# Second attention's scores stored pixel by pixel instead of neighbour by neighbour

## The chip, the cores and the metric

One core of a Trainium2 chip runs the kernel as one program. The metric is the device time of one execution in microseconds (us). A core has five engines that run side by side and meet at semaphores: TensorE (PE, matrix products; its weight loads are listed as PEld), VectorE (DVE), ScalarE (ACT), GpSimd (POOL) and SyncE (SP, which here only issues transfers).

## The reference

The input is x, 8 images of 16 x 16 pixels with 192 channels. Four blocks follow each other, each added to its own input:

1. a windowed attention (windows of 14 x 14, 12 heads of 16 channels);
2. a mixture of 8 experts over all 2048 tokens, two experts for each token;
3. the second attention, in which each pixel attends to nine neighbours;
4. a second mixture of experts.

The change touches the third. In the words of the reference, cut short:

```python
for g in range(4):                      # groups of 48 channels
    qkv = einsum('oi,bihw->bohw', qkv_w, xg[g])
    for i, dil in enumerate((1, 2, 3)): # heads of 16 channels
        kp, vp = unfold(k, 3, dil), unfold(v, 3, dil)   # nine shifted copies, zero beyond the edge
        attn = softmax(einsum('bncl,bnckl->bnlk', q, kp) * 16 ** -0.5, axis=-1)   # over the nine neighbours
        out  = einsum('bnlk,bnckl->bnlc', attn, vp)
y = stack(outs).reshape(B, H, W, C) @ proj_w.T + proj_b
```

For each pixel there are nine scores, each a dot product over 16 channels; softmax over the nine; and nine value vectors weighted by them.

## The kernel before, in words

**Layout of the second attention.** A partition holds one quarter of one image (4 rows of 16 pixels, QPIX = 64) of one group, 128 partitions in all, so one pass covers everything of one dilation. The three dilations are done in the order 3, 2, 1 (indices i = 2, 1, 0; "position" 0, 1, 2). Queries, keys and values lie as 16 channels by pixels, keys and values with a halo of rows above and below. The nine neighbours are in NEIGH, three of them (the three row offsets) to a column offset of 0, -1 and +1; for a column offset only those columns are computed that lie inside the image, so that an operation has 1024 elements for offset 0, and 960, 896 or 832 for the others at dilation 1, 2 or 3.

**Steps of one dilation**, and their engines:

- products (L1679, VectorE): query times shifted key, nine tensors of 16 channels x 64 pixels, one for each neighbour;
- channel_sums (L1795, TensorE): the 16 channels are added by 16 products with the identity matrix, into PSUM, 3 x 64 scores for each column offset;
- copy_scores (L1870, ScalarE): two copies, of 6 x 64 and 3 x 64 scores, from PSUM into the tile sc[i] of 576 numbers;
- scores (L1688 and L1690, VectorE): maximum over the nine, subtracted;
- exponentials (L1875, ScalarE): in place;
- weights (L1696, L1698, L1700, VectorE): sum over the nine, reciprocal, product;
- values (L1707, VectorE): for each neighbour, the shifted value window times its weights, repeated over the 16 channels. For dilation 3 nine such terms go straight to TensorE; for the other two, two of three terms of a column are first added on VectorE (L1737), so six go to TensorE. The terms have six buffers; a seventh waits for an older one's sum;
- neighbour_sums (L1813, TensorE): adds the terms into PSUM with the identity matrix;
- value_sums (L1881, ScalarE): copies the result into acc[i] with a pixel's 16 channels side by side, that is, writing with a step of 16 words.

**The order of the work** is written out by hand, one program for each engine, and an engine takes its instructions strictly in that order:

- VectorE: products of dilations 3 and 2, scores(2), the first column of products of dilation 1, weights(2), values(2), the other two columns of products, scores(1), weights(1), values(1), scores(0), weights(0), values(0);
- TensorE: channel_sums(2), channel_sums(1), neighbour_sums(2), channel_sums(0), neighbour_sums(1), neighbour_sums(0), then 24 filler products whose result nobody reads (L1848), then transposes (L1829) and the projection (L1842);
- ScalarE: copy_scores(2), exponentials(2), copy_scores(1), value_sums(2), exponentials(1), copy_scores(0), exponentials(0), value_sums(1), value_sums(0).

The SP queue stores acc[i] to DRAM after each value_sums, reads it all back in another order for the projection, and after that issues the loads of the second mixture's expert weights. Here position(i) = 2 - i.

Of the kernel before, what the change touches and what calls it, by code (L numbers as in the profile page):

```python
# [26 lines left out]
ALU = mybir.AluOpType  # L27
ACT = mybir.ActivationFunctionType
AX = mybir.AxisListType


P = 128
IMGS, SIDE, C = 8, 16, 192
# [50 lines left out]
def build(nc, a, out):  # L84

    ctx = ExitStack()
    with ctx:
# [3 lines left out]
        def sem(name):  # L91
            return ctx.enter_context(nc.semaphore(name))
# [51 lines left out]
        ps = ctx.enter_context(nc.psum_tensor("ps", [P, 8, 512], F32))  # L144
# [82 lines left out]
        def s_(name):  # L227
            if name not in S:
                S[name] = sem(name)
            return S[name]  # L230
# [69 lines left out]
        def block_scales(v, n, b):  # L300

            ln_refine(v, n, range(b, b + 1))
            nc.vector.scalar_tensor_tensor(offset[:, b], mv[:, b, :, 0], -1.0, rstd[:, b], ALU.mult, ALU.mult)\
                .then_inc(s_("ln_offset"), 1)
# [141 lines left out]
        for kind, b, start, end in sorted(misc_uses(), key=lambda use: use[2]):  # L446
            if start < len(FRONT):
                bank = start % 8
            else:
                bank = min((MISC, MISC + 1), key=lambda k: busy[k][0])  # L450
# [1083 lines left out]
        QPIX = QR * SIDE  # L1534
        QKV_UNITS = 12
        NEIGH = [(dy, dx) for dx in (0, -1, 1) for dy in (-1, 0, 1)]
        NN = len(NEIGH)
# [3 lines left out]
        def position(i):  # L1541

            return len(DIL) - 1 - i

        def halo(d):
            return QR + 2 * d

        def columns(d, dx):

            return max(0, -dx * d), SIDE - d * abs(dx)  # L1550
# [3 lines left out]
        for d in DIL:  # L1554
            n = HD * halo(d) * SIDE
# [15 lines left out]
        sc = [rt[:, i * NN * QPIX:(i + 1) * NN * QPIX] for i in range(3)]  # L1571
        mx1 = rt[:, 3 * NN * QPIX:3 * NN * QPIX + QPIX]
        sm1 = [rt[:, 3 * NN * QPIX + (1 + i) * QPIX:3 * NN * QPIX + (2 + i) * QPIX] for i in range(3)]
# [82 lines left out]
        def attn1_vector(v):  # L1656
            vec = nc.vector

            def shifted(t, i, n):

                d, (dy, dx) = DIL[i], NEIGH[n]
                x0, w = columns(d, dx)
                return t[i][:, :, d + dy * d:d + dy * d + QR, x0 + dx * d:x0 + dx * d + w]

            def in_columns(t, i, n):

                x0, w = columns(DIL[i], NEIGH[n][1])
                return t.rearrange("p c (y x) -> p c y x", x=SIDE)[:, :, :, x0:x0 + w]

            def products(i, col):  # L1670
                pos = position(i)
                if col == 0:
                    v.wait_ge(s_(f"q_in{i}"), 4 * 16)
                    v.wait_ge(s_(f"k_in{i}"), 4 * 16)
                if pos:
                    v.wait_ge(s_("qk_sum"), 3 * (pos - 1) + col + 1)
                x0, w = columns(DIL[i], NEIGH[3 * col][1])
                for n in range(3 * col, 3 * col + 3):
                    last = vec.tensor_tensor(in_columns(prod[:, n], i, n), q1[i][:, :, :, x0:x0 + w], shifted(k1, i, n), ALU.mult)  # L1679
                last.then_inc(s_("qk_prod"), 1)  # L1680

            def by_neighbour(s):
                return s.rearrange("p (n x) -> p n x", n=NN)

            def scores(i):
                pos = position(i)
                v.wait_ge(s_("sc_copied"), pos + 1)
                vec.tensor_reduce(mx1, sc[i].rearrange("p (n x) -> p x n", n=NN), AX.X, ALU.max).then_inc(s_("soft"), 1)  # L1688
                v.wait_ge(s_("soft"), pos + 1)
                vec.tensor_tensor(by_neighbour(sc[i]), by_neighbour(sc[i]), mx1.unsqueeze(1).broadcast_to([P, NN, QPIX]),  # L1690
                                  ALU.subtract).then_inc(s_("sc_ready"), 1)

            def weights(i):
                pos = position(i)
                v.wait_ge(s_("ex_ready"), pos + 1)
                vec.tensor_reduce(sm1[i], sc[i].rearrange("p (n x) -> p x n", n=NN), AX.X, ALU.add).then_inc(s_("norm"), 1)  # L1696
                v.wait_ge(s_("norm"), 3 * pos + 1)
                vec.reciprocal(sm1[i], sm1[i]).then_inc(s_("norm"), 1)  # L1698
                v.wait_ge(s_("norm"), 3 * pos + 2)
                vec.tensor_tensor(by_neighbour(sc[i]), by_neighbour(sc[i]), sm1[i].unsqueeze(1).broadcast_to([P, NN, QPIX]),  # L1700
                                  ALU.mult).then_inc(s_("norm"), 1)
                v.wait_ge(s_("norm"), 3 * pos + 3)

            def value_product(i, n, to):
                x0, w = columns(DIL[i], NEIGH[n][1])
                weight = sc[i][:, n * QPIX:(n + 1) * QPIX].rearrange("p (y x) -> p y x", x=SIDE)[:, :, x0:x0 + w]
                return vec.tensor_tensor(in_columns(to, i, n), shifted(v1, i, n),  # L1707
                                         weight.unsqueeze(1).broadcast_to([P, HD, QR, w]), ALU.mult)

            made, pairs = [0], [0]  # L1710

            def next_term():

                m = made[0]
                made[0] += 1
                if m >= TERMS:
                    v.wait_ge(s_("pv_sum"), m - TERMS + 1)
                return term[m % TERMS]

            def values(i):  # L1720
                v.wait_ge(s_(f"v_in{i}"), 4 * 16)
                if position(i) == 0:
                    for phase in range(3):
                        v.wait_ge(s_(f"qkv_out{phase}"), 16 * STORES)
                    for n in range(NN):
                        value_product(i, n, next_term()).then_inc(s_("pv_term"), 1)
                    return
                for col in range(3):
                    value_product(i, 3 * col + 2, next_term()).then_inc(s_("pv_term"), 1)
                    a_ = next_term()  # L1730
                    if pairs[0]:
                        v.wait_ge(s_("pv_term"), made[0] - 2)
                    value_product(i, 3 * col, a_)
                    value_product(i, 3 * col + 1, second_term).then_inc(s_("pair"), 1)
                    pairs[0] += 1
                    v.wait_ge(s_("pair"), pairs[0])
                    vec.tensor_tensor(in_columns(a_, i, 3 * col), in_columns(a_, i, 3 * col), in_columns(second_term, i, 3 * col),  # L1737
                                      ALU.add).then_inc(s_("pv_term"), 1)

            for i in (2, 1):  # L1740
                for col in range(3):
                    products(i, col)
            scores(2)
            products(0, 0)
            weights(2)
            values(2)
            products(0, 1)
            products(0, 2)
            scores(1)
            weights(1)  # L1750
            values(1)
            scores(0)
            weights(0)
            values(0)
            for u in range(2):
                vec.memset(rt[KC:KC + 1, u * 2 * BT:u * 2 * BT + BT], 1.0).then_inc(s_("y_ones"), 1)

            for b in range(BLKS):
                v.wait_ge(s_("proj1_mm"), b + 1)
                xs = x_sb[:, b * TPB:(b + 1) * TPB, :].rearrange("p (h t) c -> p h t c", h=2)  # L1760
                u = b % 2 * 2
                nc.vector.tensor_tensor(xs, xs, ps[:, u:u + 2, 0:2 * C].rearrange("p h (t c) -> p h t c", t=2), ALU.add)\
                    .then_inc(s_("proj1_out"), 1)
                v.wait_ge(s_("proj1_out"), b + 1)
                ln_moments(v, 3, range(b, b + 1))
                if b:
                    block_scales(v, 3, b - 1)
            block_scales(v, 3, BLKS - 1)
# [86 lines left out]
        def attn1_scalar(act):  # L1855
# [10 lines left out]
            def copy_scores(i):  # L1866
                pos = position(i)
                for bank, cols, count in ((SCORES[pos][0], slice(0, 6 * QPIX), 2), (SCORES[pos][1], slice(6 * QPIX, NN * QPIX), 3)):
                    act.wait_ge(s_("qk_sum"), 3 * pos + count)
                    last = nc.scalar.activation(sc[i][:, cols], ps[:, bank, 0:cols.stop - cols.start], ACT.Copy)  # L1870
                last.then_inc(s_("sc_copied"), 1)

            def exponentials(i):
# [3 lines left out]
            def value_sums(i):  # L1877
# [5 lines left out]
                    .then_inc(s_("acc_ready"), 1)  # L1883

            copy_scores(2)
            exponentials(2)
            copy_scores(1)
            value_sums(2)
            exponentials(1)
# [249 lines left out]
```

## Time and profile before

| | us |
|---|---|
| median of 3 runs (880.88 to 885.36) | 883.62 |
| the profiled execution, whole | 876.38 |
| its span | 874.6 |
| TensorE busy | 775.4 (89%) |
| VectorE busy | 419.6 (48%) |
| ScalarE busy | 308.2 (35%) |
| GpSimd busy | 363.2 (42%) |

The shares are averages over the whole program. The second attention's part from the first products of queries and keys to the last sum of values lies between 520 and 609 us of the span, and the rows are read from there. A line number (L1707) is that of the kernel; a mean is in ns, a start in us from the span's start. A busy matmul is not a TensorE at its peak, since matmuls are pipelined.

### The profile page before, as it was taken

The numbers are of one execution on the slowest core, as the hardware profiler recorded it, in microseconds if no ns is written. First come the engines' busy times: TensorE is split into PE (matmuls) and PEld (weight loads), VectorE is DVE, ScalarE is ACT, GpSimd is POOL, SyncE is SP. The second block draws the span as 40 slices with busy tenths as digits, with TensorE's granted clock in tenths as the row PEclk, the third lists the DMA queues.
The fourth block names the chain that finished last, engine by engine and source line by source line (L and its number), as shares of the span: only waits on it lengthen the run. The fifth ranks groups of instructions, "written<-read, shape, count | busy, mean of one in ns | idle before, by whom it ended". The sixth has DMA issues, their size and how long they took to land.

```text
span 874.6 us, 19316 instructions
## 1 busy us (share of the span) xinstructions
PE 775.4 (89%) x6126; PEld 660.1 (75%) x6127; DVE 419.6 (48%) x998; ACT 308.2 (35%) x858; POOL 363.2 (42%) x789
## 2 busy tenths in 40 slices
PE   8799999999987999999991589998967999999990
PEld 4577887888773999999990459783753999999980
DVE  5344455466648333333325427997347333333325
ACT  3403545555523333333340650011350333333330
POOL 8724343430132566666642030000033566666640
PEclk9855999999987999999996599999988999999995
DMA  7672565564482111111114089400980111111116
GB/s 235 189 170 79 116 171 133 138 148 89 160 334 86 46 48 49 42 51 52 47 35 145 7 252 216 68 25 28 322 336 25 43 51 46 49 48 47 49 24 216
DMA packets 60794, 96.50 MB, mean 110 GB/s; under 512 B 25679, under 2 KB 43812, under 8 KB 60744
## 3 DMA queue, kind: packets, MB, share of 16 engines
q1 hardware_dynamic: 43272, 61.56, 25.8%
q0 software_dynamic: 17472, 34.27, 13.2%
q8 instruction: 31, 0.51, 0.3%
q14 instruction: 19, 0.16, 0.1%
HBM read 65.51 MB, written 31.52 MB: 111 GB/s over the span
## 4 chain that ended last, share of the span: by engine, by line
PE 65%; DVE 15%; DMA 6%; issue 6%; POOL 4%; ACT 2%; SPq 1%; DVEq 0%; POOLq 0%
PE ps L1419 15%; PE ps L1427 11%; PE ps L1431 7%; PE ps L1795 4%; PE ps L754 3%; PE ps L779 3%; DVE x_sb L1359 2%; PE ps L730 2%; PE ps L1410 2%; PE ps L799 2%; PE ps L1813 2%; DVE arena L1707 2%; DMA kk<-kd 2%; PE ps L375 2%; PE ps L823 2%
## 5 line engine op out<-in xcount | busy, mean ns | idle before, releaser
L1461 ACT ACTIVATE arena<-ps,b1s 128x128 f32<-128x128 f32 x468 | 129.6, 375 | 254.1 <-PE ps L1431 170.2
L1419 PE MATMUL ps<-arena 128*128 x936 | 165.4, 327 | 1.5 <-DVE rt L1324 1.5
L1419 PEld LDWEIGHTS ps<-arena 128*128 128x128 f32 x936 | 150.3, 190 | 2.4 <-issue 2.1
L1427 PE MATMUL ps<-xnT 128*128 128x128 f32 x936 | 117.5, 275 | 3.8 <-DVE xnT L1317 3.8
L1427 PEld LDWEIGHTS ps<-xnT 128*128 128x128 f32 x936 | 114.4, 192 | 4.8 <-DVE xnT L1317 4.8
L272 POOL TENSOR_TENSOR rstd<-veps,cst 128x4 f32<-128x4 f32 (+1 forms) x12 | 14.9, 1239 | 189.7 <-DVE veps L266 189.6
L609 DVE TENSOR_REDUCE rt<-ps 98x2 f32<-98x392 f32 x96 | 53.2, 562 | 78.0 <-PE ps L779 78.0
L1475 POOL TENSOR_TENSOR credit<-credit 1x1 f32<-1x1 f32 x306 | 57.4, 187 | 77.0 <-DVE rt L1324 34.6
L1483 POOL DMA_INDIRECT xnT<-xnd,gcur x78 | 78.3, 1004 | 16.2 <-issue 15.2
L1026 ACT ACTIVATE arena<-ps 98x392 f32<-98x392 f32 x96 | 47.0, 499 | 76.6 <-PE ps L799 76.0
L1431 PE MATMUL ps<-xnT,rt 64*128 64x128 f32 x936 | 73.2, 289 | 0.0
L1493 POOL DMA_INDIRECT yd<-rt,scur x52 | 54.3, 1044 | 30.3 <-issue 30.3
L1331 DVE COPY xnT<-arena 128x768 f32 x78 | 44.5, 571 | 46.4 <-issue 45.6
L1431 PEld LDWEIGHTS ps<-xnT,rt 64*128 64x128 f32 x936 | 58.3, 187 | 9.4
L1317 DVE COPY xnT<-ps 128x256 f32<-128x256 f32 x78 | 33.1, 424 | 64.7 <-PE ps L1411 63.4
L1324 DVE TENSOR_TENSOR rt<-ps,xn 128x192 f32<-128x192 f32 x52 | 18.6, 358 | 82.2 <-issue 43.3
L779 PE MATMUL ps<-kk,qq 114*98 114x196 f32 x192 | 46.1, 328 | 6.4 <-DMA kk<-kd 6.2
L1795 PE MATMUL ps<-arena,cst 128*128 128x192 f32 x288 | 48.8, 333 | 3.1 <-DVE arena L1679 3.1
L1795 PEld LDWEIGHTS ps<-arena,cst 128*128 128x128 f32 x288 | 48.4, 195 | 3.9 <-DVE arena L1679 3.6
L754 PEld LDWEIGHTS ps<-xnT,arena 128*112 128x112 f32 (+2 forms) x448 | 40.0, 183 | 7.4 <-POOL xnT L554 4.1
L754 PE MATMUL ps<-xnT,arena 128*112 128x32 f32 (+4 forms) x448 | 42.2, 269 | 3.2 <-POOL xnT L554 3.2
L779 PEld LDWEIGHTS ps<-kk,qq 114*98 114x98 f32 x192 | 29.1, 189 | 16.5 <-issue 14.4
(211 smaller groups left out, 1278.6 us busy)
## 6 DMA issues: line engine op xcount, KB each, us to landing
arena<-in_w SPq DMA_DIRECT2D x16, 576.0 KB, 11.2
arena<-in_w1a SPq DMA_DIRECT2D x16, 384.0 KB, 6.0
arena<-yd SPq DMA_DIRECT2D x8, 768.0 KB, 7.1
kk<-kd SPq DMA_DIRECT2D x48, 96.0 KB
qq<-qd SPq DMA_DIRECT2D x16, 264.0 KB
qq<-qd SPq DMA_DIRECT2D x16, 192.0 KB
arena<-in_w1b SPq DMA_DIRECT2D x16, 192.0 KB, 6.3
qkvd<-arena POOLq DMA_DIRECT2D x8, 384.0 KB, 8.0
```

The lines of the kernel that those rows point to most:

```text
L609: m = nc.vector.tensor_reduce(mxa[0:WAH, cc, 2 * u:2 * u + 2, j], ps[0:WAH, SM + u, 0:2 * WA].rearrange("p (q n) -> p q n", q=2), AX.X, AL ...
L754: last = mm(o, relt[w][0:rows, at, 0:cols], q, start=True, stop=True)
L779: last = mm(ps[0:WAH, SM + u, c * WA:(c + 1) * WA], q[:, at:at + WAH], k[:, u * WA:(u + 1) * WA], start=True, stop=True)
L1026: e = nc.scalar.activation(pa[H % EXPS][0:WAH, u], ps[0:WAH, ST + n % 2, 0:2 * WA], ACT.Exp)
L1419: last = mm(ps[:, DOWN, 0:C], hidT[r][:, f, :], w2s[:, e, f, :], start=f == 0, stop=f == FT - 1)
L1427: mm(hidden(r, f), wcura[r][:, f * P:(f + 1) * P], xgT[:, 0, :], start=f < 2, stop=False, skip_group_check=True)
L1431: last = mm(hidden(r, f), wcurb[r][rows, f // 2 * P:(f // 2 + 1) * P], xgT[rows, 1, :], start=False, stop=f >= FT - 2, skip_group_check=True)
L1461: last = nc.scalar.activation(hidT[r][:, f, :], hidden(r, f), ACT.Gelu, bias=b1s[l][:, bass.ds(e * FT + f, 1)])
L1475: nc.gpsimd.tensor_tensor(credit[0:1, 12 + kind:13 + kind], credit[0:1, 0:1], credit[0:1, 0:1], ALU.add)\
L1483: nc.gpsimd.indirect_dma_start(out=xg[r], out_offset=None, in_=xnd[l], in_offset=bass.IndirectOffsetOnAxis(ap=gcur[:, r:r + 1], axis=0))\
L1493: nc.gpsimd.indirect_dma_start(out=yd[l], out_offset=bass.IndirectOffsetOnAxis(ap=scur[:, r:r + 1], axis=0), in_=ys[r], in_offset=None, bo ...
L1795: last = mm(to.rearrange("p (n x) -> p n x", n=3), ident, prod[:, 3 * col:3 * col + 3, c, :], start=c == 0, stop=c == HD - 1)
```

## The change

The tile sc[i] of 576 numbers keeps its size and place. Before, the number of neighbour n and pixel x is at n * 64 + x; after, at x * 9 + n. All that read or write it follow: ScalarE's two copies write it through a view that steps by nine words; the two reductions read nine adjacent words for each pixel; subtraction and normalisation repeat the pixel's maximum or factor nine times innermost instead of the whole row of 64 nine times; the value products read the weights of one neighbour nine words apart. The exponential runs over the whole tile as before. No instruction is added, removed or moved, and no wait is changed.

```diff
-            def by_neighbour(s):
-                return s.rearrange("p (n x) -> p n x", n=NN)
+            def by_pixel(s):
+                return s.rearrange("p (x n) -> p x n", n=NN)
...
-                vec.tensor_reduce(mx1, sc[i].rearrange("p (n x) -> p x n", n=NN), AX.X, ALU.max).then_inc(s_("soft"), 1)
+                vec.tensor_reduce(mx1, by_pixel(sc[i]), AX.X, ALU.max).then_inc(s_("soft"), 1)
                 v.wait_ge(s_("soft"), pos + 1)
-                vec.tensor_tensor(by_neighbour(sc[i]), by_neighbour(sc[i]), mx1.unsqueeze(1).broadcast_to([P, NN, QPIX]),
+                vec.tensor_tensor(by_pixel(sc[i]), by_pixel(sc[i]), mx1.unsqueeze(2).broadcast_to([P, QPIX, NN]),
                                   ALU.subtract).then_inc(s_("sc_ready"), 1)
...
-                vec.tensor_reduce(sm1[i], sc[i].rearrange("p (n x) -> p x n", n=NN), AX.X, ALU.add).then_inc(s_("norm"), 1)
+                vec.tensor_reduce(sm1[i], by_pixel(sc[i]), AX.X, ALU.add).then_inc(s_("norm"), 1)
...
-                vec.tensor_tensor(by_neighbour(sc[i]), by_neighbour(sc[i]), sm1[i].unsqueeze(1).broadcast_to([P, NN, QPIX]),
+                vec.tensor_tensor(by_pixel(sc[i]), by_pixel(sc[i]), sm1[i].unsqueeze(2).broadcast_to([P, QPIX, NN]),
                                   ALU.mult).then_inc(s_("norm"), 1)
...
-                weight = sc[i][:, n * QPIX:(n + 1) * QPIX].rearrange("p (y x) -> p y x", x=SIDE)[:, :, x0:x0 + w]
+                weight = sc[i].rearrange("p (y x n) -> p n y x", n=NN, x=SIDE)[:, n, :, x0:x0 + w]
...
-                    last = nc.scalar.activation(sc[i][:, cols], ps[:, bank, 0:cols.stop - cols.start], ACT.Copy)
+                    n0, n1 = cols.start // QPIX, cols.stop // QPIX
+                    last = nc.scalar.activation(sc[i].rearrange("p (x n) -> p n x", n=NN)[:, n0:n1],
+                                                ps[:, bank, 0:cols.stop - cols.start].rearrange("p (n x) -> p n x", n=n1 - n0),
+                                                ACT.Copy)
```

## Rows read from the trace of the kernel before

**Rows 1.** The page's chain that ended last: shares by engine, and by line.

```profile
PE 65%; DVE 15%; DMA 6%; issue 6%; POOL 4%; ACT 2%; SPq 1%; DVEq 0%; POOLq 0%
PE ps L1419 15%; PE ps L1427 11%; PE ps L1431 7%; PE ps L1795 4%; PE ps L754 3%; PE ps L779 3%; DVE x_sb L1359 2%; PE ps L730 2%; PE ps L1410 2%; PE ps L799 2%; PE ps L1813 2%; DVE arena L1707 2%; DMA kk<-kd 2%; PE ps L375 2%; PE ps L823 2%
```

**Rows 2.** That chain in order of time, 545 to 640: start, us, what.

```profile
556.32 13.65 PE ps L1813 x36
...
606.78 1.88 PE ps L1813 x4
608.66 10.30 PE ps L1848 x24
```

**Rows 3.** Stages: length, busy us (x) of PE, PEld, DVE, ACT, POOL, PEclk, DMA, GB/s.

```profile
556.00:570.00 14.00, 14.00 (x40) 7.15 (x40) 14.00 (x15) 0.35 (x2) 0.00 (x0) 1.00 0.00 0
570.00:585.00 15.00, 15.00 (x94) 15.00 (x93) 13.59 (x15) 2.90 (x3) 0.00 (x0) 1.00 0.09 36
...
598.00:608.00 10.00, 8.28 (x19) 3.53 (x20) 9.63 (x10) 0.00 (x0) 0.00 (x0) 1.00 0.13 53
```

**Rows 4.** VectorE's timeline, 540 to 610: start, us, operation, count, idle before.

```profile
547.91 3.50 DVE L1679 TENSOR_TENSOR arena<-pk,kk 128x1024 f32<-128x1024 f32 x3 [1.23 <-DMA kk<-qkvd]
551.32 1.14 DVE L1696 TENSOR_REDUCE rt<-rt 128x64 f32<-128x576 f32 x1
...
553.88 9.11 DVE L1707 TENSOR_TENSOR arena<-qq,rt 128x1024 f32<-128x1024 f32 x9
562.90 6.49 DVE L1679 TENSOR_TENSOR arena<-pk,kk 128x960 f32<-128x960 f32 x6
569.32 1.14 DVE L1688 TENSOR_REDUCE rt<-rt 128x64 f32<-128x576 f32 x1
...
575.01 3.50 DVE L1707 TENSOR_TENSOR arena<-qq,rt 128x1024 f32<-128x1024 f32 x3
...
587.94 1.14 DVE L1688 TENSOR_REDUCE rt<-rt 128x64 f32<-128x576 f32 x1
```

**Rows 5.** ScalarE's timeline, 530 to 625, columns as before.

```profile
569.99 1.95 ACT L1881 ACTIVATE arena<-ps 128x1024 f32<-128x1024 f32 x1 [13.30 <-PE ps L1813]
571.74 0.67 ACT L1875 ACTIVATE rt<-rt 128x576 f32<-128x576 f32 x1
...
585.59 0.33 ACT L1870 ACTIVATE rt<-ps 128x192 f32<-128x192 f32 x1 [4.71 <-PE ps L1795]
```

**Rows 6.** VectorE's groups by shape: busy us, mean ns, idle before and releaser.

```profile
L1707 DVE TENSOR_TENSOR arena<-qq,rt 128x1024 f32<-128x1024 f32 x9 | 10.5, 1220 | 0.1
...
L1707 DVE TENSOR_TENSOR arena<-qq,rt 128x832 f32<-128x832 f32 x6 | 5.7, 1019 | 0.0
...
L1696 DVE TENSOR_REDUCE rt<-rt 128x64 f32<-128x576 f32 x3 | 3.4, 1143 | 1.9 <-ACT rt L1875 1.9
L1688 DVE TENSOR_REDUCE rt<-rt 128x64 f32<-128x576 f32 x3 | 3.4, 1137 | 0.0
...
L1690 DVE TENSOR_TENSOR rt<-rt 128x576 f32<-128x576 f32 x3 | 2.3, 759 | 0.1
```

**Rows 7.** Groups by shape of nearby operations, VectorE's two, then ScalarE's two.

```profile
L609 DVE TENSOR_REDUCE rt<-ps 98x2 f32<-98x392 f32 x96 | 53.2, 562 | 78.0 <-PE ps L779 78.0
...
L1239 DVE TENSOR_TENSOR rt<-rt 128x128 f32<-128x128 f32 x4 | 1.2, 291 | 0.1
...
L1881 ACT ACTIVATE arena<-ps 128x1024 f32<-128x1024 f32 x3 | 5.8, 1930 | 29.5 <-PE ps L1813 29.5
...
L1870 ACT ACTIVATE rt<-ps 128x192 f32<-128x192 f32 x3 | 1.0, 332 | 14.1 <-PE ps L1795 14.1
```

**Rows 8.** Stages, for the granted clock (the number after POOL's), columns as Rows 3.

```profile
48.00:72.00 24.00, 23.61 (x106) 19.79 (x105) 8.91 (x17) 3.09 (x9) 7.74 (x10) 0.50 0.56 131
520.00:523.00 3.00, 0.17 (x1) 0.00 (x0) 3.00 (x3) 0.59 (x1) 0.52 (x1) 1.00 1.02 416
523.00:526.00 3.00, 2.69 (x8) 2.70 (x9) 3.00 (x5) 0.00 (x0) 0.00 (x0) 0.51 1.03 418
```

## The prediction

> **What bounds the kernel now.** I read four views in order: the chain of waits, the same chain in order of time around the second attention, a table of busy time by stage there, and VectorE's own timeline. The chain as a whole is a TensorE chain (65%), with VectorE at 15%, and the value products' line L1707 is only 2% of it [rows 1]. That share says little about this change: the time of one stage counts. In the stage the chain names TensorE until 569.97 us [rows 2] and then goes over mostly to VectorE, until the last TensorE sum at 606.78 us. The table shows why the chain's naming must be read with care: from 556 to 570 us both TensorE and VectorE are busy for 14.00 of 14.00 us [rows 3], so there are two chains side by side, and the one on VectorE is the one that goes on: its next instruction, L1688 at 569.32, follows its products without a gap [rows 4], and does not wait for the TensorE sums that end at 569.97. From 570 to 608 us VectorE is busy for 13.59 of 15 and 9.63 of the last 10 us [rows 3], and its only wait there for another engine is for ScalarE's exponential, 1.9 us in all [rows 6]. So VectorE, from L1696 at 551.32 to the last addition at about 606.75, is one string of work with almost no slack. What is added to it is added to the kernel.
>
> **What the change does to each operation.** The scores (576 numbers per partition: 9 neighbours by 64 pixels) are now stored pixel by pixel.
>
> *The two reductions.* Before, each reads a pixel's nine scores 64 words apart: 1.14 us for 576 elements [rows 6]. The nearest reduction in sequence, L609, takes 562 ns for 392 elements (out of PSUM, which is why I allow it 0.02 us either way) [rows 7], and the two shapes of L1707 give VectorE's rate: (1220 - 1019) / 192 = 1.047 ns an element [rows 6]. 576 in sequence: 562 + 184 x 1.047 = 755 ns. Each reduction loses 0.39 us, and the strided read is priced by the same rows: (1140 - 755) / 576 = 0.67 ns an element more.
>
> *Subtraction and normalisation.* The broadcast operand now has its repeat innermost. L1239 compares 128 elements with an operand repeated eight times innermost, in 291 ns; from L1690 (759 ns for 576) down at 1.047 ns an element, 128 elements would be 290 ns [rows 6, 7]. So no change: 0.76 us stays. Bounds: 0 both ways to within 0.01 us. The exponential runs over 576 adjacent numbers before and after: 0.
>
> *ScalarE's copies of the scores* now write with a step of nine words. The nearest row is L1881, which writes with a step of 16 words: 1930 ns for 1024, where its rate for adjacent writes, 332 ns for 192 and 0.83 ns each, gives about 1025; 0.88 ns an element more [rows 7]. The last copy of each attention (192 elements) grows by 0.17 us, the first by 0.34 us. All are covered: VectorE comes to the scores of dilation 1 at 587.94, and the copy ended at 585.92 [rows 4, 5]; the other two copies have more cover. These 2.0 us grow if VectorE gets later. Cost 0; without cover 0.17 us each.
>
> *The value products.* 27 of them, each a multiplication of a shifted value window by the weights of one neighbour, repeated over 16 channels: 9 of 1024 elements and 6 each of 832, 896 and 960. They run at 1.22 us for 1024 and 1.02 us for 832, 1.05 ns an element beyond the fixed part [rows 6], with odd and even window offsets alike. After the change the weights are nine words apart, every element a jump. No row of before has VectorE reading with such a step in one of two operands. Bounds: below, 0 (the second operand's port hides it, since its words are used again for each channel); above, the ScalarE row's 0.88, and since no row tells what a small step costs VectorE, I leave room up to twice the reduction's price, 1.34 ns an element. I take 0.67 ns, that of the reduction's row, because it is the only row of the same engine, reading, with jumps that leave no two adjacent words. The elements: dilation 3 comes first with 3 x 1024 + 6 x 832 = 8064, then dilation 2 with 8448, then dilation 1 with 8832; together 25,344. Extra: 5.4 + 5.7 + 5.9 = 17.0 us.
>
> The Trainium skill, page "Vector Engine (DVE) Microarchitecture Reference", section 5.2 (Measured stream behaviour on trn2), says the same of the mechanism: a port keeps its full rate only on runs of at least two adjacent words, and one source that jumps at every element makes it 1.73 ns instead of 1.054. It also says that small non-adjacent steps cost more than large ones, with 2.50 ns for steps of 24 words in both sources; no row here shows that for VectorE. By that figure, my estimate from the page would be an extra of 1.45 ns an element and 36.7 us instead of 17.0.
>
> **The sum along VectorE's string.** Scores of dilation 3: the reduction's gain is lost, because products(0, 0) behind it waits for a transfer until 547.91 anyway [rows 4]. Weights of dilation 3: -0.39; products +5.40, their end moves from 562.90 to 567.9. Here TensorE sums the terms at about 1.5 us each from 556.3 on and finishes at 569.97 [rows 2]; the last term now arrives at 567.9 and its sum takes 1.4 to 1.5 us, so TensorE still ends at about 570 and channel_sums(0) is not late. The six products behind, which the weights don't touch, shift by 5.0 us: the next scores start at 574.3 instead of 569.32. There -0.39 for each of two reductions, and ScalarE's exponential, which started at 571.74 right behind the value copy of 569.99 to 571.94 although its input was ready at 571.25 [rows 5], finds ScalarE free: -0.45. Products of dilation 2: +5.66. Scores and weights of dilation 1: -0.78. Products of dilation 1: +5.92. Total 16.98 - 5 x 0.39 - 0.45 = +14.6 us at the last addition. The wait for a free buffer of the six terms never bites: the sums it asks for are older than two terms.
>
> **What is late next: TensorE's clock.** The sums now wait for VectorE. Between the last term of dilation 2 (597.4) and the first of dilation 1 (603.7) TensorE has work for 1.9 us and then nothing for about 4. After 3.1 us of nothing, at 520.17 to 523.30, the granted clock went from 1.00 to 0.51 (from 2.4 to 1.2 GHz) [rows 8]. At 1.2 GHz the last sum (four matmuls, 1.88 us [rows 2]) would take some 1.6 us more, and the 24 filler matmuls behind it (10.30 us) up to 1.5 us more if the clock comes back as it did after 526; if it had come back before, nothing. I take 1.0 us between 0 and 3.1. From the last sum on, ScalarE's copy, the stores and reloads through DRAM, the projection and the whole second mixture of experts follow and shift without change; the SP queue that loads the expert weights stands behind the reload of the values, so no transfer starts early.
>
> Sum: +14.6 + 1.0 = +15.6 us. The profiled execution took 876.38 us (span 874.6 and 1.8 around it): 892.0. The median of the three runs is 883.62, 7.2 above the profiled one; I expect the same offset, so 883.62 + 15.6 = 899.2 us.
>
> **Rivals.**
>
> *The small step costs more than the large one (25%).* For it: in this trace ScalarE's step of 16 words costs 0.88 ns an element while VectorE's step of 64 costs 0.67, two engines, so the step itself is not separated; against: no VectorE row has it. With 0.88 the products cost 22.3 us and the kernel +20.9, 904.5; with twice the reduction's price, 34.0 us and +32.6, 916.2. Every other step of the sum stays. By the figure for steps of 24 words on the Trainium skill's page named above it would be +35.3, an estimate again.
>
> *The weight port hides the step, not slower than before (8%).* Place: L1707. The weights of a channel are the same 64 words 16 times over and only one of three streams jumps. If this costs nothing, what is left are the reductions, -0.39 three times: the gain on scores(1) is eaten by ScalarE's copy until 571.94 [rows 5], so -0.39 for the weights there and -0.78 for dilation 1. The last addition moves by -1.2, and the time is 882.4: not slower. The point from which it decides: with less than 0.05 to 0.09 ns an element (1.2 to 2.4 us over 25,344) there is no loss, and with less than about 0.25 ns none that a measurement can tell. Against it: the reduction has one stream that jumps too, and pays.
>
> *TensorE hides the first part (4%).* Reading the chain of waits literally, the products of dilation 3 are off it and their 5.0 us are free: +10.6, 894.2. Against: VectorE is 14.00 of 14.00 us busy there [rows 3].
>
> *TensorE's clock stays low through the sums and the fillers (8%).* From 48 to 72 us it was granted 0.50 although TensorE was busy for 23.61 of 24 us [rows 8], so it does not always come back at once. Then the last sum costs 1.6 and the fillers 10.3 more instead of 1.0: +26.5, 910.1.
>
> **How the numbers follow.** Forecast 55%, the four rivals as above. A change of under 0.5% (4.4 us) can't be told from none by a measurement of this kernel. Only the hidden port leads there, and part of an intermediate price: same 0.09. Nothing gives a gain of 4.4 us (all that the edit can save is 2.4 to 3): faster 0.01. Slower 0.90. The range begins at 890 (0.67 cut to a half, or a lower median) and ends at 919, so that it holds nearly all of the price up to twice the row.
>
> **What would show it.** L1707 rows of 1024 elements at about 1.91 us and of 832 at 1.58; L1688 and L1696 at 0.75; L1690 and L1700 unchanged; L1870 at 0.83 and 0.50; VectorE without a gap from 551 to about 621; L1848 starting near 623 instead of 608.66, and granted clock under 1.00 at some place between 600 and 610. Wrong if L1707 keeps 1.22 us (hidden port) or takes over 2.2 us (step price), or if the last sum moves by another amount than VectorE's own busy time grows by.

## The result

The changed kernel takes 898.14 us (median of 4 runs, 889.22 to 900.03), the one before 882.25 (875.02 to 885.36): ratio 1.0188, 95% interval 1.0136 to 1.0240. Timed again beside other runs of the kernel before it was 897.22 (6 runs), ratio 1.0201 (1.0154 to 1.0248). The ratios of 1.019 and 1.020 are some 17 us; forecast were +15.6 us and 899.2.

### The profile page after: what moved, and what is told of

It is laid out like the page before. It is cut to its first block, busy times and chain, and to the rows that moved or that the text cites. A ratio compares the mean times of both kernels' runs of the same rounds, so it can differ in the third digit from the quotient of the medians.

```text
span 896.7 us, 19316 instructions
## 1 busy us (share of the span) xinstructions
PE 789.8 (88%) x6126; PEld 667.0 (74%) x6127; DVE 435.9 (49%) x998; ACT 310.3 (35%) x858; POOL 364.3 (41%) x789
## 4 chain that ended last, share of the span: by engine, by line
PE 60%; DVE 17%; issue 6%; DMA 6%; POOL 5%; SPq 3%; ACT 2%; DVEq 0%; POOLq 0%
PE ps L1419 14%; PE ps L1427 10%; PE ps L1431 7%; DVE arena L1707 4%; PE ps L754 3%; DVE x_sb L1359 2%; PE ps L779 2%; PE ps L730 2%; PE ps L1410 2%; SPq L1606 2%; PE ps L375 2%; PE ps L799 2%; PE ps L823 2%; DMA qkvd<-arena 1%; PE ps L865 1%
## 5 line engine op out<-in xcount | busy, mean ns | idle before, releaser
L1813 PE MATMUL ps<-arena,cst 128*128 128x512 f32 (+3 forms) x84 | 38.9, 610 | 14.8 <-DVE arena L1737 11.7
L1707 DVE TENSOR_TENSOR arena<-qq,rt 128x1024 f32<-128x1024 f32 (+3 forms) x27 | 48.1, 1848 | 0.1
```

## The profile after

The profiled execution took 898.54 us, its span 896.7. First VectorE's groups by shape in the changed kernel, in the columns of [rows 6] and against them.

```profile
L1707 DVE TENSOR_TENSOR arena<-qq,rt 128x1024 f32<-128x1024 f32 x9 | 17.5, 2002 | 0.1
L1707 DVE TENSOR_TENSOR arena<-qq,rt 128x960 f32<-128x960 f32 x6 | 10.9, 1870 | 0.0
...
L1707 DVE TENSOR_TENSOR arena<-qq,rt 128x896 f32<-128x896 f32 x6 | 10.3, 1775 | 0.0
L1707 DVE TENSOR_TENSOR arena<-qq,rt 128x832 f32<-128x832 f32 x6 | 9.5, 1668 | 0.0
...
L1690 DVE TENSOR_TENSOR rt<-rt 128x576 f32<-128x576 f32 x3 | 2.3, 758 | 0.1
...
L1688 DVE TENSOR_REDUCE rt<-rt 128x64 f32<-128x576 f32 x3 | 2.3, 752 | 0.0
L1696 DVE TENSOR_REDUCE rt<-rt 128x64 f32<-128x576 f32 x3 | 2.3, 751 | 1.5 <-ACT rt L1878 1.5
```

The value products grew from 1220 to 2002 ns for 1024 elements and from 1019 to 1668 for 832. With 1151 and 1084 ns before for 960 and 896 elements the sum is 9 x 0.782 + 6 x (0.719 + 0.691 + 0.649) = 19.4 us over 25,344 elements: 0.765 ns an element. The reductions fell to 0.75 us, the elementwise operation kept 758 ns. ScalarE's copies of the scores, its two groups:

```profile
L1871 ACT ACTIVATE rt<-ps 128x384 f32<-128x384 f32 x3 | 2.6, 872 | 23.2 <-PE ps L1795 23.2
...
L1871 ACT ACTIVATE rt<-ps 128x192 f32<-128x192 f32 x3 | 1.6, 525 | 13.0 <-PE ps L1795 13.0
```

The groups of the kernel before that [rows 6] and [rows 7] leave out, for both comparisons:

```profile
L1707 DVE TENSOR_TENSOR arena<-qq,rt 128x960 f32<-128x960 f32 x6 | 6.6, 1151 | 0.0
L1707 DVE TENSOR_TENSOR arena<-qq,rt 128x896 f32<-128x896 f32 x6 | 6.2, 1084 | 0.0
...
L1870 ACT ACTIVATE rt<-ps 128x384 f32<-128x384 f32 x3 | 1.5, 492 | 26.5 <-PE ps L1795 26.5
```

The copies grew by 0.38 and 0.19 us, 1.0 ns an element. Now VectorE's timeline of the changed kernel, in the columns of [rows 4].

```profile
551.87 3.50 DVE L1679 TENSOR_TENSOR arena<-pk,kk 128x1024 f32<-128x1024 f32 x3 [1.74 <-DMA kk<-qkvd]
555.28 0.74 DVE L1696 TENSOR_REDUCE rt<-rt 128x64 f32<-128x576 f32 x1
...
557.44 15.26 DVE L1707 TENSOR_TENSOR arena<-qq,rt 128x1024 f32<-128x1024 f32 x9
572.60 6.51 DVE L1679 TENSOR_TENSOR arena<-pk,kk 128x960 f32<-128x960 f32 x6
579.01 0.76 DVE L1688 TENSOR_REDUCE rt<-rt 128x64 f32<-128x576 f32 x1
...
581.31 0.75 DVE L1696 TENSOR_REDUCE rt<-rt 128x64 f32<-128x576 f32 x1 [0.75 <-ACT rt L1878]
...
583.48 5.86 DVE L1707 TENSOR_TENSOR arena<-qq,rt 128x1024 f32<-128x1024 f32 x3
...
605.17 0.75 DVE L1696 TENSOR_REDUCE rt<-rt 128x64 f32<-128x576 f32 x1 [0.75 <-ACT rt L1878]
```

I measure the stage from the start of weights(2), L1696, to the start of the last sum of values. Before it ran from 551.32 [rows 4] to 606.78 [rows 2], 55.46 us. The chain in order of time of the changed kernel ends it at 627.55:

```profile
557.44 15.26 DVE arena L1707 x9
...
627.55 1.88 PE ps L1813 x4
629.43 10.30 PE ps L1848 x24
```

627.55 - 555.28 = 72.27 us, 16.8 more. The chain now goes through L1707 at 557.44 in one piece, where before it went through TensorE's sums: the string that was off the chain on the page has become the chain. The last sum (1.88 us) and the fillers (10.30 us) are as long as before [rows 2]. Within the stage VectorE waits for another engine only at ScalarE's exponentials of dilations 2 and 1, 0.75 us each (1.20 and 0.75 before), and never for TensorE.

The two profiled spans lie 22.1 us apart, more than the stage explains. Of the rest 4.0 us lie ahead of weights(2) (555.28 against 551.32), where nothing was changed, and 1.3 behind the last sum (269.2 against 267.8 us to the end). The second profile of the kernel before, below, has its weights(2) at 555.54, so the 4.0 us are spread between executions and not the change's. The 1.3 us are a spell of low TensorE clock that other kernels of this set have too, as told below.

## The experiments

All stages are as defined above. Timed ratios are against the kernel before on the same chip.

**Value products read adjacent words.** In the changed kernel:

```diff
-                weight = sc[i].rearrange("p (y x n) -> p n y x", n=NN, x=SIDE)[:, n, :, x0:x0 + w]
+                weight = sc[i][:, n * QPIX:(n + 1) * QPIX].rearrange("p (y x) -> p y x", x=SIDE)[:, :, x0:x0 + w]
```

> The changed kernel, but the value products read 64 adjacent words of the scores tile (so each neighbour gets the wrong weights; nothing else is left out). Stage from the start of weights(2), its reduction, to the start of the last sum: 55.46 us before, 72.27 after. Theory (all of the loss is VectorE's nine-word step in the value products): L1707 back at 1.22 us for 1024, stage 54.3 us (the reductions' gain, 0.39 three times), kernel 1 us under the one before, ratio 0.999. Rival (ScalarE's slower copies or a lower TensorE clock carry part of the loss): stage over 56 us and the kernel slower than before by 2 us or more.

VectorE's and then TensorE's timeline of this kernel give the ends of the stage:

```profile
547.92 0.74 DVE L1696 TENSOR_REDUCE rt<-rt 128x64 f32<-128x576 f32 x1
```

```profile
602.29 1.88 PE L1813 MATMUL ps<-arena,cst 128*128 128x480 f32 x4 [0.91 <-DVE arena L1737]
```

The products are back at 1221 ns for 1024 elements, and the stage is 602.29 - 547.92 = 54.37 us: the whole loss is gone, with ScalarE's slower copies still in place, so the copies carry no part of it. The five reductions inside the stage save 1.95 us; 0.84 of it goes to a longer wait for the exponential of dilation 2 (2.04 us instead of 1.20), and 1.1 is left. This run does not separate TensorE's clock, which did not fall inside its stage; that the clock carries no part of the stage follows from the changed kernel's timeline above, in which VectorE never waits for TensorE. The total did not follow: ratio 1.0070 (1.0038 to 1.0103) over 12 runs, which on its face is the rival's number. The excess does not lie in the stage: from the start of the last sum to the end it took 277.9 us instead of 267.8. The stages of this kernel behind the projection (granted clock is the number after POOL's):

```profile
630.00:632.00 2.00, 0.10 (x1) 0.00 (x0) 1.97 (x6) 1.89 (x5) 0.48 (x1) 1.00 1.03 413
...
634.00:652.00 18.00, 18.00 (x81) 17.23 (x79) 0.51 (x4) 6.18 (x13) 5.83 (x8) 0.50 0.81 301
```

After a pause of TensorE of 1.93 us (to 632.03) the clock fell to 0.50 (from 2.4 to 1.2 GHz) and stayed there for 18 us in which TensorE was busy for 18.00.

**The same kernel and the one before, profiled again.**

> The changed kernel with the value products reading adjacent words (wrong weights), once more: its stage was 54.4 us, 1.1 under the one before, yet 12 timed runs were 0.4 to 1.0% over it. In its profile TensorE's granted clock was 0.50 from 632 to 662 us although TensorE was busy all the time, and from the start of the last sum to the end it took 277.9 us instead of 267.8. Theory (whether that low clock falls there differs from execution to execution of one kernel): stage again 54.4, the rest again between 267 and 279, not necessarily 278. Rival (a fixed cost of this kernel): 277.9 within 0.5.

> The kernel before, profiled once more. Theory (the stage is fixed by VectorE's string, what lies ahead of it and behind it moves with the clock): stage 55.5 us within 0.7, start of weights(2) anywhere from 548 to 556 us, the rest from the last sum 267 to 278. Rival (the parts outside the stage are fixed for this kernel): 551.3 and 267.8 again.

The stages were 53.7 and 55.3 us, the rest 274.4 and 267.9, and weights(2) began at 547.32 and 555.54. The stage repeats; the first one is 0.7 us shorter than in this kernel's first profile because the wait for the exponential was 1.39 us and not 2.04. What lies ahead moves by 4 us, as expected. The rest of the first kernel, 274.4, lies in the range of the theory (267 to 279) and not at the rival's 277.9, with a granted clock of 0.50 once more from about 631.4 us, for some 13 us. For the kernel before, the rival's 267.8 came again and its 551.3 did not.

The spell belongs to no single kernel. From the end of the fillers to the end of the span it took 255.6 to 255.8 us in seven of the twelve profiles of this document. In the other five it took 257.0 (changed kernel, first profile), 258.7 (ScalarE turns the weights, below), 262.2 and 265.7 (this kernel), and 265.8 (the first run on steps, below). In these five the clock fell at the same pause of TensorE, 1.93 us long and some 30 us behind the start of the last sum; in the seven it stayed at 1.00 over that pause. Two falls in two profiles, worth 6.6 and 10.1 us, would account for a timed ratio of 1.007 with a shorter stage, but no timed run outside a profile shows its stages. What decides whether the clock falls there is open, and the timed ratio of this kernel says nothing about the stage.

**Only the value products read with the step.** In the kernel before, the same line the other way round:

```diff
-                weight = sc[i][:, n * QPIX:(n + 1) * QPIX].rearrange("p (y x) -> p y x", x=SIDE)[:, :, x0:x0 + w]
+                weight = sc[i].rearrange("p (y x n) -> p n y x", n=NN, x=SIDE)[:, n, :, x0:x0 + w]
```

> The kernel before, with only the value products reading with a step of nine (so the weights are permuted; nothing else is left out). Theory: L1707 at 2.00 us for 1024 and 1.67 for 832 as in the changed kernel, 19.4 us more of VectorE; stage 55.5 + 19.4 - 0.45 (ScalarE free for the exponential of dilation 2) = 74.4 us, ratio to before 1.021. If the price came from the whole new layout and not from this read alone, L1707 would be under 2 us and the stage under 72.

```profile
L1707 DVE TENSOR_TENSOR arena<-qq,rt 128x1024 f32<-128x1024 f32 x9 | 17.4, 1994 | 0.1
...
L1707 DVE TENSOR_TENSOR arena<-qq,rt 128x832 f32<-128x832 f32 x6 | 9.5, 1651 | 0.0
...
L1696 DVE TENSOR_REDUCE rt<-rt 128x64 f32<-128x576 f32 x3 | 3.4, 1138 | 1.5 <-ACT rt L1875 1.5
```

The groups by shape show the products as slow as in the changed kernel, with the reductions at their old 1.14 us. Stage 629.77 - 555.62 = 74.15 us, ratio 1.0264 (1.0219 to 1.0309). The read alone is the price; the layout's other edits only take 1.9 us off it. The ratio is higher than the 1.021 expected. Against the first profile of the kernel before, the span is 24.6 us longer: 4.3 us lie ahead of weights(2), 18.7 in the stage, and 1.7 in the last sum, at a clock of 0.50, and the fillers, which ended 13.87 us after its start instead of 12.18. How the timed runs divide is not known.

**Only ScalarE's copies write with the step.** In the kernel before, copy_scores of the changed one.

> The kernel before, with only ScalarE's two score copies writing with a step of nine (softmax then works on permuted scores; nothing else is left out). Theory: copies of 0.87 and 0.53 us instead of 0.49 and 0.33, all hidden: stage 55.5 us, ratio 1.000. Rival (they hold up the scores): stage 55.9 us or more.

Copies of 0.88 and 0.53 us, ratio 0.9977 (0.9931 to 1.0023), stage 56.1 us, which is the rival's side by my own bound. The trace puts the 0.6 us elsewhere: TensorE's sums of dilation 3 began 5.44 us after weights(2) here, 4.83 before and 4.65 in its second profile, all set by when the transfers of keys arrived. Where VectorE is quick, its exponential of dilation 2 waits for ScalarE, and ScalarE for those sums. The copies themselves ended 1.8 us or more before VectorE came for them. VectorE's wait for that exponential was 1.65 us (1.20 and 1.01 in the two profiles before) and the products of dilation 3 took 9.26 us instead of 9.11, which makes up the 0.6. So the bound was too tight, and no wait for the copies is seen.

**Only dilation 3 reads with the step.** In the changed kernel, behind the line of the weights:

```diff
+                if i < 2:
+                    weight = sc[i][:, n * QPIX:(n + 1) * QPIX].rearrange("p (y x) -> p y x", x=SIDE)[:, :, x0:x0 + w]
```

> The changed kernel with the step of nine in the value products of dilation 3 alone; dilations 2 and 1 read 64 adjacent words (wrong weights there). Theory (VectorE's string sets the end although TensorE is busy all the time): extra 3 x 0.78 + 6 x 0.65 = 6.2 us of products, less 5 x 0.39 and 0.45: stage 59.3 us, 3.8 over before, ratio 1.005. Rival (TensorE's sums of dilation 3 hide them, as the chain of waits has it): stage 54.3 us, ratio 0.999.

VectorE's timeline of it:

```profile
552.53 0.74 DVE L1696 TENSOR_REDUCE rt<-rt 128x64 f32<-128x576 f32 x1
...
569.85 6.48 DVE L1679 TENSOR_TENSOR arena<-pk,kk 128x960 f32<-128x960 f32 x6
576.26 0.73 DVE L1688 TENSOR_REDUCE rt<-rt 128x64 f32<-128x576 f32 x1
```

The products of dilation 3 take 15.2 us instead of 9.0 (553.88 to 562.90 in [rows 4]), and the next scores start 23.7 us after weights(2), before 18.0. TensorE was busy all that time, its sums of dilation 3 took 14.4 us instead of 13.65, and none of it hid VectorE's 5.7 us: stage 611.71 - 552.53 = 59.18 us, ratio 1.0036 (0.9996 to 1.0076). Both chains ran side by side, and the one off the printed chain was the one that counted.

**What a step costs.** In the kernel before, the 27 products read x instead, each with a step of its own:

```diff
+                def stepped(k):
+                    return flat[:, 0:QPIX * k].rearrange("p (y x k) -> p k y x", k=k, x=SIDE)[:, 0, :, x0:x0 + w]\
+                        .unsqueeze(1).broadcast_to([P, HD, QR, w])
...
+                if (i, n) == (1, 1):
+                    return vec.tensor_tensor(out_, in_, stepped(4), ALU.mult)
```

> The kernel before, with the 27 value products reading their weights from x instead of the scores, each with its own step: for 1024 elements steps of 1, 2, 3, 4, 8, 9, 16, 24 words and pairs of adjacent words 18 apart; for the narrower shapes 1, 2, 3, 4, 5, 6, 8, 9, 12, 16, 24, 32, 48. Theory A (any read that leaves no adjacent pair costs the same): all steps from 2 on cost 0.7 to 0.8 ns an element, pairs nothing. Theory B (the distance matters, small steps cost more, as the step of 64 words cost the reduction 0.67 and the step of nine 0.77): a slope or bumps over the steps, with 24 words at 1 ns or more. Theory C (what counts is whether two successive reads fall in one group of four words): steps of 2 free or half price, 3 in between, 4 and above full price.

Groups of 1024 elements, from the top with steps of 24, 4, 9, 16, 3 and 2 words:

```profile
L1759 DVE TENSOR_TENSOR arena<-qq,x_sb 128x1024 f32<-128x1024 f32 x1 | 2.7, 2711 | 0.0
...
L1739 DVE TENSOR_TENSOR arena<-qq,x_sb 128x1024 f32<-128x1024 f32 x1 | 2.0, 2029 | 0.0
...
L1755 DVE TENSOR_TENSOR arena<-qq,x_sb 128x1024 f32<-128x1024 f32 x1 | 2.0, 1981 | 0.0
...
L1757 DVE TENSOR_TENSOR arena<-qq,x_sb 128x1024 f32<-128x1024 f32 x1 | 1.9, 1873 | 0.0
...
L1737 DVE TENSOR_TENSOR arena<-qq,x_sb 128x1024 f32<-128x1024 f32 x1 | 1.6, 1579 | 0.0
...
L1716 DVE TENSOR_TENSOR arena<-qq,x_sb 128x1024 f32<-128x1024 f32 x1 | 1.2, 1218 | 0.0
```

A step of two words is free, three words cost 0.35 ns an element, four 0.79. That is theory C for the small steps; theory A falls with steps 2 and 3, and theory B has only the dear step of 24 for it. For both runs on steps there is one execution each, and the means are read, not the totals.

> The kernel before, with the value products reading their weights from x (so the values are wrong; nothing is left out): full-width products (1024 elements) in pairs of words, given as first word and distance inside the pair, pairs 16 words apart: (0,1), (3,1), (0,2), (0,3), (1,1), (2,2), and steps of 20, 28, 40; the narrower ones with steps 7 to 47. Theory (VectorE pays 0.6 to 0.8 ns an element unless two successive reads fall in one aligned group of four words): (0,1), (0,2), (0,3), (1,1) free at 1.22 us, (3,1) and (2,2) 1.9 us or more. Rival (adjacent pairs on an even word are what counts): (0,1) alone free, (0,2) and (0,3) at full price, (1,1) about 0.25 ns. For the steps: 24 is alone in being dear, or all of 20 to 28 are.

Here the pairs decided. A pair is written as first word and distance, so (3,1) reads words 3 and 4. Groups of 1024 elements, from the top: step 20; pairs (2,2), (3,1), (0,3), (1,1).

```profile
L1758 DVE TENSOR_TENSOR arena<-qq,x_sb 128x1024 f32<-128x1024 f32 x1 | 2.3, 2279 | 0.0
...
L1744 DVE TENSOR_TENSOR arena<-qq,x_sb 128x1024 f32<-128x1024 f32 x1 | 2.0, 1970 | 0.0
...
L1724 DVE TENSOR_TENSOR arena<-qq,x_sb 128x1024 f32<-128x1024 f32 x1 | 1.9, 1946 | 0.0
...
L1740 DVE TENSOR_TENSOR arena<-qq,x_sb 128x1024 f32<-128x1024 f32 x1 | 1.2, 1227 | 0.0
L1742 DVE TENSOR_TENSOR arena<-qq,x_sb 128x1024 f32<-128x1024 f32 x1 | 1.2, 1226 | 0.0
```

Words 0 and 3 of an aligned group of four, and words 1 and 2, cost nothing, as do (0,1) and (0,2) at 1224 and 1216 ns; words 3 and 4, adjacent but in two groups, cost 0.71 ns an element. So two successive reads in one aligned group of four words (16 bytes) run at full rate, adjacent or not, and reads that each open a new group pay. The step of three fits: of four successive reads three open a new group, halfway between the free pairs (two of four) and the full price (four of four), and it cost 0.30 to 0.35, about half of 0.71. How much depends on the distance, from both kernels and the shapes they have (ns an element over the adjacent read):

```
step in words   1, 2   3          4 to 12      14    16         18    20         21 to 23     24         25    26
extra ns        0.00   0.30-0.35  0.74-0.79    0.70  0.64-0.66  0.75  0.86-1.03  1.07-1.12    1.18-1.46  1.14  0.96
step in words   28         30    32    36    40         44    47, 48
extra ns        0.79-0.87  0.83  0.74  0.76  0.88-0.91  0.79  0.71
```

The Trainium skill bears on both: "SBUF — State Buffer" (section Specifications (TRN2), the row on cachelines) has lines of 16 bytes that want at least two hits, and the pairs agree; "Vector Engine (DVE) Microarchitecture Reference", section 5.2, has adjacent pairs on an even word as the condition, and the free pairs (0,3) and (1,1) contradict it. Its 2.50 ns for steps of 24 words in both sources is reached here with one stepped source at 1024 elements, 1.047 + 1.455 = 2.50; at 960 elements the same step gives 1.047 + 1.18 = 2.23.

**ScalarE turns the weights back.** In the changed kernel, with a second tile wt of 576 words that the value products read adjacent:

```diff
                 nc.scalar.activation(sc[i], sc[i], ACT.Exp, scale=HD ** -0.5).then_inc(s_("ex_ready"), 1)
+                act.wait_ge(s_("ex_ready"), position(i) + 1)
+                nc.scalar.activation(wt.rearrange("p (n x) -> p n x", n=NN), sc[i].rearrange("p (x n) -> p n x", n=NN),
+                                     ACT.Copy).then_inc(s_("ex_turned"), 1)
...
+                v.wait_ge(s_("ex_turned"), pos + 1)
+                rows_ = wt.rearrange("p (n x) -> p n x", n=NN)
+                vec.tensor_tensor(rows_, rows_, sm1[i].unsqueeze(1).broadcast_to([P, NN, QPIX]), ALU.mult)
```

> The changed kernel, but after each exponential ScalarE copies the 576 exponentials into a second tile in the old order (read with a step of nine, written adjacent), while VectorE sums and inverts; VectorE then normalises that tile and the value products read it adjacent. Theory: L1707 at 1.22 us, reductions at 0.75, the turning copy takes 1.0 to 1.25 us on ScalarE and lies beside the reduction and the reciprocal (1.33 us), so the stage is 54.3 us or a little over, 1.2 under before, ratio 0.999: the gain without the price, too small for the total time to show. Rival: the copy is slower than the 1.33 us it is hidden by, and the stage is not under 55.5.

The timeline of its dilation 1, both engines:

```profile
593.73 0.68 ACT L1881 ACTIVATE rt<-rt 128x576 f32<-128x576 f32 x1 [2.99 <-DVE rt L1691]
...
594.44 1.25 ACT L1883 ACTIVATE rt<-rt 128x576 f32<-128x576 f32 x1
594.44 0.75 DVE L1697 TENSOR_REDUCE rt<-rt 128x64 f32<-128x576 f32 x1 [0.75 <-ACT rt L1881]
...
595.23 0.55 DVE L1699 RECIPROCAL rt<-rt 128x64 f32<-128x64 f32 x1
...
595.82 0.76 DVE L1703 TENSOR_TENSOR rt<-rt 128x576 f32<-128x576 f32 x1
```

The turning copy ends at 595.69, the reciprocal at 595.78: hidden by 0.1 us. Stage 610.22 - 555.73 = 54.49 us, 1.0 under the one before, and ratio 0.9997 (0.9958 to 1.0037). The best layout of both is worth one microsecond, which the total does not show.

**The changed kernel again.**

> The changed kernel once more, for a closer ratio. Its stage grew by 16.8 us, while the profiled executions lie 22.1 us apart. Theory (the rest is spread between executions, most of it ahead of the change): stage again 72.3 us, ratio 1.019, between 1.017 and 1.021. Rival (the change also costs some 5 us elsewhere): ratio 1.025.

Stage 72.24 us, ratio 1.0201, as expected. But TensorE's timeline differs from the first profile:

```profile
626.46 3.05 PE L1813 MATMUL ps<-arena,cst 128*128 128x480 f32 x4 [2.86 <-DVE arena L1737]
629.30 11.03 PE L1848 MATMUL ps<-cst 128*128 128x512 f32 x24
```

The last sum took 3.05 us instead of 1.88, and the fillers ended 640.33 - 626.46 = 13.87 us after it began; before it was 618.96 - 606.78 = 12.18 [rows 2], and in the first profile after 12.18 too. So the lower clock reached the last sum here and cost 1.7 us, as it did in the run with the products alone.

## Why the prediction was right, and where it was off

*VectorE as one string.* Right: stage +16.8 us for 19.4 us of products less what was saved, and the run with dilation 3 alone excludes the rival of the hidden first part (3.7 us over before, none hidden).

*The price of the step.* The mechanism was right and the size too small: 0.67 ns an element from the reduction's step of 64, measured 0.765 at nine words, 19.4 instead of 17.0 us. This is the term of the sum that was mis-sized. The measured price lies midway between the 0.67 taken and the 0.88 of the rival of the dear small step, so that rival had the sign right: nine words cost more than 64. But nine words lies on the plateau from 4 to 12, and what is dear, 0.9 to 1.5 ns, is a band around 24 words. The rival of the hidden port is out.

*The savings.* Right: 0.39 us for each reduction (1.14 to 0.75), the first one lost before the transfer of 551.87, and the 0.45 us at ScalarE's exponential, which found its engine free. 19.4 - 5 x 0.39 - 0.45 = 17.0, measured 16.8.

*ScalarE's copies.* Priced at 0.83 and 0.50 us, measured 0.87 and 0.53, and hidden as said.

*TensorE's clock.* The step of the forecast that was least right. The stages of the changed kernel between the sums, in the columns of [rows 8]:

```profile
603.00:606.00 3.00, 2.98 (x4) 1.17 (x4) 2.18 (x4) 0.68 (x1) 0.00 (x0) 0.50 0.00 0
606.00:608.00 2.00, 0.33 (x1) 0.00 (x0) 1.93 (x3) 1.63 (x1) 0.00 (x0) 0.96 0.00 0
...
610.00:613.00 3.00, 3.00 (x4) 0.67 (x2) 3.00 (x2) 0.00 (x0) 0.00 (x0) 0.50 0.35 142
613.00:616.00 3.00, 1.59 (x5) 0.68 (x4) 2.97 (x3) 0.00 (x0) 0.00 (x0) 1.00 0.00 0
...
627.00:640.00 13.00, 12.45 (x32) 5.79 (x33) 1.47 (x3) 1.89 (x1) 0.00 (x0) 1.00 0.34 112
```

The clock fell to 0.50 twice, in or behind pauses of TensorE of 2.72 and 3.06 us as its timeline has them (pauses of 2.90 and 2.86 us further on left it at 1.00):

```profile
603.02 3.31 PE L1813 MATMUL ps<-arena,cst 128*128 128x448 f32 x4 [2.72 <-DVE arena L1737]
609.39 3.64 PE L1813 MATMUL ps<-arena,cst 128*128 128x512 f32 x4 [3.06 <-DVE arena L1707]
614.44 3.67 PE L1813 MATMUL ps<-arena,cst 128*128 128x512 f32 x8 [1.41 <-DVE arena L1737]
```

The forecast had one pause of about 4 us in their place. But the clock was back before the last sum, and the cost there was 0 in the first profile; in the second one, and in the run with the products alone, it was 1.7 us. The 1.0 that I took lies between, and was no constant. Low clock in the sums themselves cost nothing, because TensorE waits for VectorE there.

*The total.* +14.6 and +1.0 were forecast; +16.8 and 0 to 1.7 came. The two errors add to 1 to 3 us of 16. That the median, 898.14, lies only 1.1 us from the 899.2 forecast is in part luck: the four runs spread over 10.8 us, and the difference of the medians, 15.9 us, is less than the 16.8 us by which the stage alone grew.

## What to carry to other kernels

When two layouts compete, count the elements on each side: here 3,456 elements of reductions were made adjacent and 25,344 elements of products were not. A chain of waits names one engine where two are busy throughout; look at which one's next instruction follows without a gap, since that one prices the change. On VectorE keep two successive reads of 32-bit data inside one aligned group of four words (seen here for multiplications of which one source steps); if a transposition is needed, give it to an engine that waits anyway.

## What was not expected of the hardware

A read with a step of two words cost VectorE nothing, and neither did jumps between pairs of any kind that lie inside one aligned group of four words, while steps from 20 to 26 words cost up to 1.46 ns an element more than an adjacent read, about twice what a step of 16 or of 48 costs. ScalarE paid about 0.98 ns an element for reading with a step of nine (1246 ns for the copy of 576, against 684 for the exponential that reads and writes the same 576 adjacent), as much as for writing with it. And TensorE's granted clock, which had already been at 0.50 through busy time in [rows 8], stayed there for 18 us in which TensorE was busy without a break, behind a pause of 1.93 us that other executions passed at 1.00; the execution with a stage 1.1 us shorter then ended 5.6 us later (span 880.2 against 874.6).
